# A three-layer graph kernel: layer 1 splits both neighbour tiles in every second pair, ScalarE copies its gather indices, and gathers cover 104 partitions

## The reference

```python
def sage(h, w_self, w_neigh, b):
    agg = jax.ops.segment_sum(h[src], dst, num_segments=n) * inv_deg
    return h @ w_self + agg @ w_neigh + b
h = jnp.maximum(_layernorm(x, axis=-1), 0.0)
h = jax.nn.relu(sage(h, ws0, wn0, b0))     # 128 -> 256
h = jax.nn.relu(sage(h, ws1, wn1, b1))     # 256 -> 256
h = sage(h, ws2, wn2, b2)                  # 256 -> 128
x = x + h
```

## Time and profile before

| | |
|---|---|
| Time, median of 3 runs | 3935.56 us (3934.75 to 3937.95) |
| Profiled execution, its own time | 3934.27 us |
| Its span, first to last instruction | 3932.1 us |
| Busy share PE, PEld, DVE, ACT, POOL | 89%, 81%, 90%, 77%, 58% |
| DMA packets, data moved | 1040774, 727.06 MB |
| Extraction loop, DVE | 48.32 to 124.8 us |
| Layer 0, POOL's first gather | 137.58 us |
| Layer 1, POOL's first gather | 2165.40 us |
| Layer 2, POOL's first gather | 3235.60 us |

### The profile page before, as it was taken

The page is one execution under the profiler, slowest core; times in us unless marked ns, Lnnn a source line. Parts: engine busy times, 40 slices in busy tenths (PEclk is TensorE's granted clock), DMA queues, the critical chain, the costliest instruction groups (busy, mean ns, idle before and its releaser), DMA issues. The chain is left out here.

```text
span 3932.1 us, 111274 instructions
## 1 busy us (share of the span) xinstructions
PE 3513.3 (89%) x22511; PEld 3171.6 (81%) x22511; DVE 3546.8 (90%) x12529; ACT 3016.1 (77%) x8011; POOL 2277.0 (58%) x2513
## 2 busy tenths in 40 slices
PE   0499999999999999999999899999999987776666
PEld 0488888888888888888888799999999986666565
DVE  8899999999999999999998788888888877777777
ACT  2488888888888888888886778778778767777777
POOL 1344444444444444444442777777777767777776
PEclk9999999999999999999999999999999996666666
DMA  1144444444444444444444788888888878999998
GB/s 55 56 142 139 141 143 142 139 140 144 142 140 140 143 142 139 140 144 141 139 140 139 215 244 246 244 246 247 242 243 244 242 223 256 264 264 266 265 263 251
DMA packets 1040774, 727.06 MB, mean 185 GB/s; under 512 B 103208, under 2 KB 1012656, under 8 KB 1040632
## 3 DMA queue, kind: packets, MB, share of 16 engines
q1 hardware_dynamic: 854298, 569.93, 48.2%
q0 software_dynamic: 80848, 104.93, 10.7%
q10 hardware_dynamic: 105600, 51.92, 4.4%
HBM read 451.60 MB, written 360.71 MB: 207 GB/s over the span
## 5 line engine op out<-in xcount | busy, mean ns | idle before, releaser
L581 POOL DMA_INDIRECT loaded_rows<-in_x,gather_at x784 | 859.2, 1096 | 1047.6 <-ACT h_nbr L691 906.5
L1269 PE MATMUL ps_out<-w_hi,hid_hi 128*128 128x512 f32 (+1 forms) x3136 | 1120.6, 357 | 29.9 <-DVE layer_mem L1173 28.2
L1269 PE MATMUL ps_out<-w_hi,hid_lo 128*128 128x512 f32 (+1 forms) x3136 | 1066.3, 340 | 0.0
L1269 PE MATMUL ps_out<-w_lo,hid_hi 128*128 128x512 f32 (+1 forms) x3136 | 1061.9, 339 | 0.0
L595 POOL DMA_INDIRECT layer_mem<-p_rows,gather_at x784 | 804.1, 1026 | 289.2 <-issue 216.0
L1269 PEld LDWEIGHTS ps_out<-w_hi,hid_hi 128*128 128x128 f32 x3136 | 590.8, 188 | 139.4 <-issue 39.7
L1269 PEld LDWEIGHTS ps_out<-w_hi,hid_lo 128*128 128x128 f32 x3136 | 588.7, 188 | 72.5
L1269 PEld LDWEIGHTS ps_out<-w_lo,hid_hi 128*128 128x128 f32 x3136 | 592.8, 189 | 60.7
L608 POOL DMA_INDIRECT layer_mem<-z_rows,gather_at x528 | 525.8, 996 | 181.3 <-issue 140.8
L721 ACT ACTIVATE cat_hi<-ps_turn 128x512 fp32r<-128x512 f32 x392 | 236.0, 602 | 375.3 <-PE ps_turn L1306 373.9
L1269 PE MATMUL ps_hid<-cat_hi,w_hi 128*128 128x256 f32 x1568 | 472.0, 301 | 0.0
(11 more groups left out here) (162 smaller groups left out, 8783.6 us busy)
## 6 DMA issues: line engine op xcount, KB each, us to landing
p_rows<-stored_rows SPq DMA_DIRECT2D x392, 256.0 KB, 2.2
q_rows<-layer_mem SPq DMA_DIRECT2D x392, 256.0 KB, 2.6
loaded_rows<-q_rows SPq DMA_DIRECT2D x392, 256.0 KB
loaded_rows<-y_rows SPq DMA_DIRECT2D x264, 192.0 KB
layer_mem<-in_x SPq DMA_DIRECT2D x264, 192.0 KB
out_rows<-stored_rows ACTq DMA_DIRECT2D x264, 192.0 KB
loaded_rows<-in_x SPq DMA_DIRECT2D x392, 128.0 KB, 2.6
z_rows<-layer_mem SPq DMA_DIRECT2D x392, 128.0 KB
```

The lines of the kernel that those rows point to most:

```text
L581: pool.indirect_dma_start(raw[s.slot][:, 2 + j, :], None, table, bass.IndirectOffsetOnAxis(gather_at[s.slot][:, j:j + 1], axis=0), bounds_ ...
L1269: ins = nc.tensor.matmul(o, a, b, start=n == 0, stop=n == len(terms) - 1)
```

## The change

`ROUNDS` goes from 14 to 13, so that a tile has 104 slots, and the gathers of layers 0 and 1 name 104 partitions in place of 128; layer 2's stay as they are. In layer 1, pairs of even number have both tiles split, pairs of odd number the first tile alone as before. The copy of layer 1's index columns moves from DVE to ACT, where it stands first in a step, in front of the distance; its wait for the earlier gather moves with it.

```diff
-ROUNDS = 14
-L1_SPLIT = 1
+ROUNDS = 13
+SLOT_ROWS = 8 * ROUNDS
+L1_SPLIT = (2, 1)
...
-                        pool.indirect_dma_start(rows_in[s.slot][:, j, 0:width], None, table,
-                                                bass.IndirectOffsetOnAxis(gather_at[s.slot][:, j:j + 1], axis=0),
+                        pool.indirect_dma_start(rows_in[s.slot][0:SLOT_ROWS, j, 0:width], None, table,
+                                                bass.IndirectOffsetOnAxis(gather_at[s.slot][0:SLOT_ROWS, j:j + 1], axis=0),
...
-            def layer1(first):
+            def layer1(ahead):
+                if ahead.live():
+                    if ahead.has(SLOTS):
+                        act.wait_ge(L1.gathered[ahead.slot], ahead.use * 32)
+                    act.activation(gather_at[ahead.slot][:, 0:2], slot_index[:, bass.ds(ahead.n * 2, 2)], ACT.Copy
+                                   ).then_inc(L1.index_copied, 1)
+                first = ahead.back(4)
...
-                nbr_hi_part(L1, first, L1_SPLIT, H)
+                nbr_hi_part(L1, first, L1_SPLIT[first.half], H)
...
-            pipeline(act, layer1, PAIRS, 5, rounds=3)
+            pipeline(act, layer1, PAIRS, 9, rounds=4)
...
             def layer1(first):
-                copies_index(first)
-                nbr_lo_part(L1, first.back(4), L1_SPLIT, H)
-                s = first.back(5)
+                nbr_lo_part(L1, first, L1_SPLIT[first.half], H)
+                s = first.back(1)
...
-            pipeline(dve, layer1, PAIRS, 9, rounds=4)
+            pipeline(dve, layer1, PAIRS, 5, rounds=3)
...
-                        if j < L1_SPLIT:
+                        if j < L1_SPLIT[s.half]:
```

More of the change, by code:

```diff
@@ L215, in build @@
         nbr = [part(2, H) for i in range(SLOTS)]
-        nbr_hi = [sb(f"nbr_hi{i}", [P, L1_SPLIT, H], FP32R) for i in range(2)]
-        nbr_lo = [sb(f"nbr_lo{i}", [P, L1_SPLIT, H], FP32R) for i in range(2)]
+        nbr_hi = [sb(f"nbr_hi{i}", [P, L1_SPLIT[i], H], FP32R) for i in range(2)]
+        nbr_lo = [sb(f"nbr_lo{i}", [P, L1_SPLIT[i], H], FP32R) for i in range(2)]
         gather_at = [sb(f"gather_at{i}", [P, SHARED], I32) for i in range(SLOTS)]
@@ L564, in general, with layer0_gathers @@
                         pool.wait_ge(ge_index_set, 1)
-            def layer0_gathers(table):
+            def layer0_gathers(table, rows):
                 def step(first):
@@ L580, in step @@
                         for j in range(2):
-                            pool.indirect_dma_start(raw[s.slot][:, 2 + j, :], None, table,
-                                                    bass.IndirectOffsetOnAxis(gather_at[s.slot][:, j:j + 1], axis=0),
+                            pool.indirect_dma_start(raw[s.slot][0:rows, 2 + j, :], None, table,
+                                                    bass.IndirectOffsetOnAxis(gather_at[s.slot][0:rows, j:j + 1], axis=0),
                                                     bounds_check=last_row, oob_is_err=False
@@ L616, in _ @@
             with pool.If(pool.value_load(general_flag[0:1, 0:1], min_val=0, max_val=1) != 0):
-                layer0_gathers(h0_sums)
+                layer0_gathers(h0_sums, P)
             with pool.Else():
-                layer0_gathers(x)
+                layer0_gathers(x, SLOT_ROWS)
             for q in range(SLOTS):
@@ L1019, in general @@
                         dve.wait_ge(ge_nodes_set, 2)
[L1021 to L1028, removed]
             def nbr_lo_part(layer, s, tiles, width):
```

## The result

The changed kernel takes **3984.69 us** in the median of four runs (3982.01 to 3985.6), against 3936.35 for the kernel before beside it: a ratio of 1.0122, 95% interval 1.0104 to 1.0139. It is slower by 1.2%. The forecast was 3931, with a range of 3905 to 3965.

A forecast was written before the change was run, and what follows sets the result against it. POOL's gathers were taken to pace layer 1, 1.00 us each with 0.30 gaps. Extraction -5.7, 104 partitions 0, split 0 and stall +1 made about -5 us: 3931 us from a median of 3935.56, range 3905 to 3965.

The forecast's parts named there:

- 104 partitions: POOL's gather issue in layers 0 and 1: 104 rows give shares of 8, so still 1.00 us a gather, 0 us.
- since one rule fits both rows: Reason for 0 us: issue cost follows rows per engine's share, 0.018 us each, fitting gathers of 114 and 128 rows.
- rival C: Layer 1's 784 issues: a share count other than 16 costs POOL in itself; 0.05 us gives 3969, 0.20 gives 4087; 18%.
- by both the sum keeps 0 here: Gathers: 13 engines with 8 rows each by the skill's rule, or the packet count; either way the term is 0 us.
- While POOL paces, that lateness is absorbed: Layer 1: copy and distance put 0.9 us between a landing and `nbr_hi`, through to POOL's buffer; claimed to cost nothing.
- rival D: Layer 1's buffer loop closes, POOL waiting for the sum four pairs back; 0.1 us a pair is 39 us, about 3970; 4%.
- The stall: Layer 1: DVE's subtraction delays gathers whose start it covers; change open from -23 to +25 us, taken as +1.
- Thirteen rounds: Extraction on DVE, where everything waits for it: one round fewer saves all its time, -5.7 us.
- POOL paces layer 1: Rival A, the forecast: POOL still paces layer 1, gathers at 1.00 us and gaps of 0.30; 3907 to 3955 us; 62%.
- the split alone: Layer 1's even pairs: PE saves 0.22 us each, 0.11 on average; buys 0 us under POOL's pace, otherwise 43 us.
- Layer 0 covers its dearer gathers: Layer 0: POOL's 1.3 us of waiting per gather covers even +0.20 us a gather.
- ACT's copy: Layer 1's index copy on ACT: 0.19 to 0.29 us, making ACT's step 2.46 to 2.56 us, hidden under 2.60.

The follow-up runs named there:

- the two combinations above: Twelve rounds and 96 rows, once with split and ACT's late copy, once without split and copy on DVE; on slow-SyncE chips, 1.0021 and 1.003 of the kernel before.
- f4_96_split: Kernel before with twelve rounds, 96-row gathers in layers 0 and 1, and the even-pair split, copy left on DVE; 3907.23 us against 3935.28, 0.9925.
- e9_rows104b: Kernel before with only the gathers of layers 0 and 1 over 104 partitions, on a slow-SyncE chip; 4354.03 us against 4362.95, 0.9978.
- g1_96_late: Kernel before with twelve rounds, 96 rows, the split, and ACT's copy behind `nbr_hi`, on a slow-SyncE chip; 4408.96 us against 4398.82, 1.0021.

## Why the prediction was wrong

**The step that failed** is "*104 partitions* ... **0 us**", and in it the reason "since one rule fits both rows". A gather of 114 rows took 1.20 us and one of 128 took 1.00; the prediction laid all of the 0.20 on the share of 19 rows against 8. That split was chosen, not shown, as rival C said. The counts on either side of 128 part the two causes: a number of engines other than 16 costs 0.08 us in itself (104 against 128, both 8 rows to an engine: 1.082 and 0.998), and the remaining 0.12 for 11 further rows is 0.011 us a row. That second price is only rough: 96 against 128 gives 0.031 for 2 rows, and 126 rows, with 9 to an engine, cost 0.007 less than 104. The term is 784 x 0.084 = +66 us where 0 was written. It is rival C, which had 18%; its sentence with 0.05 us gave 3969, and with the measured 0.084 it gives 3935.6 + 66 - 5.7 = 3996. The result is 11 lower, mostly by the smaller stall.

The packets were read rightly and answered another question: 80848 before and after says that surplus engines get descriptors too, and the sizes of the packets show it for 114 rows: the seven gathers made 630 packets of 8 bytes, nine for each of the ten engines without rows. By the Trainium skill's rule (DMA: Bandwidth & Descriptors, "Why a DMA increments its semaphore by 16 and not by 1") 104 rows go to 13 engines; the packet count is in keeping with it, but would be the same with 16. A count of packets doesn't say what POOL pays for writing them: "by both the sum keeps 0 here" was true of the transfer and not of the issue.

**The second error** is "While POOL paces, that lateness is absorbed", and with it the 4% for rival D. The lateness itself was right to the tenth: 0.9 us forecast, 0.92 measured from landing to `nbr_hi`. But at 2.60 us a pair there was no room for it. Alone the copy costs +18.0 us and with the split +26.7. In both, POOL is idle longer (30.6 and 23.9 us), most of it behind the sum four pairs back. The prediction had looked at the gaps of before and seen 0.30 everywhere but before the first; ten are longer, seven of them the rare ones. That nearly all are 0.30 shows that the loop had slack, not how much. In the kernel before the sum ends 1.86 us (median) ahead of the gather that needs its buffer, but under 1.05 in one case of twenty, and 0.89 of it is needed: 0.97 of slack as a rule and 0.16 at times, against a shift of 0.9. In the changed kernel the median is still 1.55, where the copy by itself leaves 0.99: the dearer gathers stretch the period, and only 25 of the buffer's gaps are long, by 3.3 us in all. That is why the parts don't add: +54.2 (104 rows) and +26.7 (copy and split) would make 80.9, and together they make 56.5. On top of the first loss the second costs only 2.3 us.

**The stall**: +1 us was taken between -23 and +25; it was -13.5 with the whole change, -6.6 with 104 rows alone and +2.0 without them. Before, 115 gathers of layer 1 were over 30 ns longer than at rest, and after, 39. It depends on where in the period the subtraction falls, as was said; the size was not to be had from the trace of before. Its cause, two inputs in SBUF, was taken rightly.

**What held.** Thirteen rounds: -5.28 us for -5.7, and -10.9 for two rounds. POOL paces layer 1 at 77% busy while PE shows 972 us of 1000: the split alone changes nothing. Layer 0 covers its dearer gathers (31.4 us more busy time, 32.5 less idle) and layer 2 is untouched. ACT's copy costs 0.20 us (0.19 to 0.29 forecast). That PE's busy share fell 5% for a forecast 4 is luck: the split was to do it, and it was the longer pair that did. The split alone takes 2% off, half of what was reckoned.

**What stays open**: the cause of the step of 0.084 inside POOL's work of issuing, which is not the number of packets, the rare gaps of POOL, the two combinations above, and SyncE's slowness on some chips, which is read from the trace and on which nothing was changed by experiment.

## What to carry to other kernels

Where an engine is seldom idle for more than its fixed gap it paces, whatever its busy share; price one instruction of it with a row of exactly the new shape, and where the nearest row differs in two things, keep both causes at their full size. Trim an indirect gather to a multiple of 16 rows: of the counts tried here 96 and 112 are cheaper than 128, and 104, 120 and 126 dearer. A share of busy time can fall because the period grew, so reckon it by the pair. Before putting work in front of the first reader of a landing, compare its length with the smallest slack of the buffer loop, and if it is longer, put the work behind that reader.

## What the runs showed of the hardware

- A gather's issue on POOL, lowest of each: 0.96 us for 96 rows, 0.98 for 112, 0.99 for 128; 1.08 for 104 and 120, 1.07 for 126.
- POOL answers a semaphore that it waits for late: from the end of PE's sum, as the trace models it, to the start of the gather it releases it is 0.89 us (0.91 with 96 rows, 0.97 with 104), where back to back gathers are 0.30 apart.
- Apart from that, POOL has a gap of 0.67 to 2.0 us before every 108th gather of layer 1 in the kernel before, and of 2.0 to 3.1 before every 122nd with 96 rows (label f4_96_split).
- A DVE operation with two inputs in SBUF that runs over the start of a gather stalls its issue, by up to 0.35 us under 256 columns, and it is the same for `tensor_tensor` and `scalar_tensor_tensor` (804.1 and 806.3 us busy). With one of the inputs in PSUM the same operation stalls none of 525. The Trainium skill (SBUF — State Buffer, "Who interferes with whom") states that a DVE instruction with two SBUF inputs contends with a GpSimd instruction that reads SBUF; these traces agree.
- On three of the chips one and the same program takes 11 to 12% longer, with SyncE's register moves in layer 1 at 0.15 us on average (label e9_rows104b) in place of 0.029. In that kernel the granted TensorE clock was 1.00 between 2300 and 3100 us, as on the usual chips; in label g1_96_late it was 0.94.
